# Nine layer norms in fp16 parts transposed by DMA, and the dense weight split early, in a one-core transformer block

## The chip, the core and the metric

The kernel runs on one core of a Trainium2 chip: TensorE (PE in the rows, its weight loads PEld), VectorE (DVE), ScalarE (ACT), GpSimd (POOL), and SyncE (SP), which here only issues DMAs. The metric is device time in microseconds (us) of one execution, as the median of several.

## The reference, cut to what matters

```python
def _layernorm(x): return (x - mean(x)) / sqrt(var(x) + 1e-5)
def _binary_diff_weight(w, base): d = w - base; return base + mean(abs(d)) * sign(d)
def ffn(h):   # W1, W3: [1792, 512], W2: [512, 1792], each from _binary_diff_weight
    return (silu(h @ W1.T) * (h @ W3.T)) @ W2.T
x = x + 0.5 * ffn(_layernorm(x))          # x: [2, 1024, 512] float32
x = x + attn(_layernorm(x))               # qkv, rope, causal softmax, dense; 32 heads, 8 kv heads of 16
x = x + 0.5 * ffn(_layernorm(x))
```

## The kernel before

The 2048 tokens are 16 tiles of 128 rows, in 4 chunks of 512. Every layer norm of a chunk has a number n: 0 to 3 feed the chunks of the first FFN, 4 to 7 the qkv projection, 8 to 11 the second FFN. Float32 products are made of three fp16 products (`PASSES`), each operand being a high part (the value rounded to fp16) and a low part (what the rounding left).

A norm goes like this. `norm_stats` on VectorE makes mean and 1/sigma of four token tiles (four `BN_STATS` and some 17 tiny steps). `normalised` writes four tiles `xnorm` in float32, a token on each partition. The products need the features on the partitions, so `ln_transpose` on TensorE transposes each tile by four 128x128 products with `ident` into PSUM; `ln_hi` on ScalarE casts a bank to the high part in `xt`, `ln_lo` on VectorE subtracts it and writes the low part.

A step t of an FFN chunk (14 of them, `IT`) is `gate(t)`, `up(t)` and then `down(t-1)` on TensorE, 12 products each. ScalarE follows with `silu` and `h_hi`, VectorE with `product` and `h_lo`. The next chunk's norm stands between these: stats and `normalised` after step 1, the transposes around the gate of step 12; norms 4, 5 and 6 lie around steps 4, 8 and 12 of the first FFN's last chunk (`LN_AT`).

The qkv stage loops over 16 token tiles. TensorE makes `qkv(i)` into one of two PSUM pairs; `take_raw(i)` on ScalarE empties it, and TensorE waits for that of tile i-2 before tile i. GpSimd makes `rot_s` (the sine half of the rotation), VectorE `along(i)` (the cosine half), `add_turned(i)` and `low_parts(i)`, ScalarE `high_parts(i)`. Norm 7 sits in this loop: its stats after pass 2 of VectorE's loop, `normalised` after pass 4, transposes ahead of `qkv(6)` and `qkv(7)`. SyncE then transposes q and k parts by DMA into `qa` and `ka` (`place_operands(g)`), in program order on its one queue.

Attention is a hand-written order over 16 groups g and periods k: `score_piece(k, r)` on TensorE and `reduce_piece(k, r)` on VectorE find each row's maximum of group k (25 pieces), the transposed maxima are copied to `mrow` (`take_rowmax`) and four DMAs put them as rows into `qa`, and one and two periods later the scores of that group, with `exps` on ScalarE and `values` on TensorE. TensorE's `scores_t(g, 0, 0)` waits for the four `mrow` DMAs (`m_placed`).

The dense weight is loaded behind the operands of group 2 (`wd_raw`), its largest magnitude taken by ScalarE in period 0 (`dense_magnitude`), reduced over partitions by GpSimd (`dense_bound`), turned into a power of two by VectorE between pieces 16 and 17 of period 0 (`dense_scale`), its high parts cast by ScalarE (`dense_high`), its low parts subtracted by GpSimd (`dense_low`); four DMAs `wd_at` to `wd` follow in period 7, on SyncE between `place_operands(10)` and the `mrow` DMAs of group 8.

Of the kernel before, what the change touches and what calls it, by code (L numbers as in the profile page):

```python
# [123 lines left out]
def build(nc, x_in, w1t, m1t, w3t, m3t, w2t, m2t, wqkvt, b_qkv, wdt, b_d, cos_in, sin_in, out):  # L124
# [143 lines left out]
    lnt_full = sem("lnt_full")  # L268
    xhi_ready, xlo_ready = sem("xhi_ready"), sem("xlo_ready")
# [18 lines left out]
    wd_scaled, wd_unit, wdhi_ready, wdlo_ready, wd_placed = (  # L288
        sem("wd_scaled"), sem("wd_unit"), sem("wdhi_ready"), sem("wdlo_ready"), sem("wd_placed"))
# [43 lines left out]
    LN_AT = {4: 4, 8: 5, 12: 6}  # L333

# [22 lines left out]
    def _(sp):  # L357
# [35 lines left out]
        sp.dma_start(bq[:, :], b_qkv.partition_broadcast(P)).then_inc(tables_loaded, 16)  # L393

# [15 lines left out]
        sp.wait_ge(lnt_full, 8 * TPC)  # L410
# [6 lines left out]
        sp.dma_start(wd_raw[:, :, :], wdt.rearrange("(t p) n -> p t n", p=P)).then_inc(wd_loaded, 16)  # L417
        sp.dma_start(bd[:, :], b_d.partition_broadcast(P)).then_inc(wd_loaded, 16)
# [1594 lines left out]
```

## Time and profile before

| | |
|---|---|
| time, median of 3 | 1526.37 us (1523.14 to 1528.73) |
| the profiled execution: its time, its span | 1523.47 us, 1521.7 us |
| TensorE busy | 1428.3 us, 94% of the span |
| VectorE, ScalarE, GpSimd busy | 57%, 40%, 11% |
| mean granted TensorE clock | 0.977 of full speed |
| first FFN from its chunk 1; qkv; attention; second FFN | from 154.5, 489.5, 571.1, 1073.9 us |

A share of busy time is a mean over stages. TensorE is busy throughout both FFNs; between 571 and 632 us it is busy in part only, at half clock.

### The profile page before, as it was taken

What the parts mean: (1) busy time and instruction counts of PE and PEld (TensorE: products, weight loads), DVE (VectorE), ACT (ScalarE), POOL (GpSimd) and SP (SyncE); (2) the same over time, 40 slices, a digit from 0 to 9 for tenths busy, and PEclk for the clock granted to TensorE, in tenths of its full rate; (3) what the DMA queues carried; (4) which work ended last, traced back from release to release, by engine and by line L of the source; (5) the groups of instructions that cost most, each with busy time, mean ns of one, the idle gap of its engine ahead of it and who ended that gap; (6) DMA issues with size and microseconds to landing.
All of it is one profiled execution on the core that took longest, in us unless ns stands there. A gap on an engine that the chain in (4) does not pass through costs nothing.

```text
span 1521.7 us, 24288 instructions
## 1 busy us (share of the span) xinstructions
PE 1428.3 (94%) x9136; PEld 628.1 (41%) x9136; DVE 865.0 (57%) x1362; ACT 601.9 (40%) x852; POOL 167.8 (11%) x251
## 2 busy tenths in 40 slices
PE   1999999999999993799999999999999999999998
PEld 0444444444444451233333333334444444444443
DVE  7998414413453766899998999945412412412212
ACT  5862112212221452477777778753212112112111
POOL 1000000000000650233332222210000000000000
PEclk9999999999999995699999999999999999999999
DMA  9605500000000013011112111024000000000000
GB/s 387 224 0 191 234 0 1 0 0 1 1 0 1 1 30 75 1 31 27 28 28 61 26 28 26 2 98 194 0 0 0 28 0 1 28 0 1 28 0 28
DMA packets 64136, 68.88 MB, mean 45 GB/s; under 512 B 52016, under 2 KB 52016, under 8 KB 63536
## 3 DMA queue, kind: packets, MB, share of 16 engines
q1 hardware_dynamic: 64048, 67.67, 13.1%
q8 instruction: 60, 0.98, 0.3%
q14 instruction: 28, 0.23, 0.1%
HBM read 40.63 MB, written 15.20 MB: 37 GB/s over the span
## 4 chain that ended last, share of the span: by engine, by line
PE 88%; DVE 4%; issue 3%; SPq 2%; DMA 1%; ACT 1%; POOL 0%; DVEq 0%; ACTq 0%; POOLq 0%
PE ps L1504 38%; PE ps L1525 17%; PE ps L1743 9%; PE ps L1657 6%; PE ps L1724 5%; PE ps L1644 4%; PE ps L1841 3%; PE ps L1551 2%; PE ps L1498 1%; PE ps L1753 1%; DVE rowmax L1332 1%; DMA w_raw<-w1t 1%; PE ps L1661 1%; SPq L403 1%; SPq L399 1%
## 5 line engine op out<-in xcount | busy, mean ns | idle before, releaser
L803 ACT ACTIVATE probs<-ps 128x1024 f32<-128x1024 f32 (+3 forms) x384 | 292.2, 812 | 85.1 <-PE ps L1724 83.5
L1504 PE MATMUL ps<-xt_hi,w_all 128*128 128x512 f16 x896 | 275.3, 380 | 9.3 <-DVE w_all L1011 9.3
L1332 DVE TENSOR_REDUCE rowmax<-ps 128x2 f32<-128x1024 f32 (+3 forms) x208 | 237.4, 1142 | 12.4 <-PE ps L1665 5.9
L1657 PE MATMUL ps<-ka,qa 48*128 48x512 f16 (+3 forms) x768 | 162.6, 347 | 36.8 <-DVE rowmax L1332 22.6
L1166 DVE SCALAR_TENSOR_TENSOR hb<-ps,scal,silub 128x512 f32<-128x512 f32 x56 | 42.0, 750 | 267.4 <-PE ps L1504 267.4
L1504 PE MATMUL ps<-xt_lo,w_all 128*128 128x512 f16 x448 | 170.5, 381 | 0.0
L1743 PE MATMUL ps<-probs,vs 128*32 128x512 f32 (+3 forms) x1536 | 165.4, 502 | 2.4 <-ACT ctx_sb L822 2.4
L1336 DVE TENSOR_REDUCE rowmax<-ps 128x1 f32<-128x512 f32 x192 | 131.1, 683 | 8.1 <-PE ps L1657 8.1
L1504 PEld LDWEIGHTS ps<-xt_hi,w_all 128*128 128x128 f16 (+1 forms) x896 | 87.9, 98 | 115.1 <-issue 11.4
L1724 PE MATMUL ps<-qa,ka 50*128 50x512 f16 (+3 forms) x768 | 131.8, 331 | 3.2 <-DMA qa<-mrow 2.3
L1525 PE MATMUL ps<-w32b_all,hhib 128*128 (+1 forms) x448 | 133.3, 379 | 0.0
L1166 DVE SCALAR_TENSOR_TENSOR ha<-ps,scal,silua 128x512 f32<-128x512 f32 x42 | 31.5, 751 | 153.5 <-PE ps L1504 153.5
L715 ACT ACTIVATE silub<-ps,scal 128x512 f32<-128x512 f32 x56 | 38.5, 687 | 197.9 <-PE ps L1504 197.9
L536 POOL TENSOR_SCALAR_AFFINE_SELECT probs<-probs 128x512 f32<-128x512 f32 x128 | 81.6, 637 | 309.5 <-ACT probs L803 309.5
L1657 PEld LDWEIGHTS ps<-ka,qa 48*128 48x128 f16 x768 | 48.9, 95 | 154.0 <-DVE rowmax L1332 84.2
L1525 PE MATMUL ps<-w_all,hhia 128*128 128x512 f16 (+1 forms) x336 | 100.0, 379 | 0.0
L722 ACT CAST hhib<-hb 128x512 f16<-128x512 f32 x56 | 34.6, 617 | 157.8 <-DVE hb L1166 157.8
L1525 PE MATMUL ps<-w32b_all,hlob 128*128 (+1 forms) x224 | 84.9, 379 | 0.0
L715 ACT ACTIVATE silua<-ps,scal 128x512 f32<-128x512 f32 x42 | 28.9, 687 | 140.4 <-PE ps L1504 140.4
L722 ACT CAST hhia<-ha 128x512 f16<-128x512 f32 x42 | 25.9, 617 | 117.2 <-DVE ha L1166 117.2
L1504 PE MATMUL ps<-xt_hi,w32b_all 128*128 128x512 f16 x224 | 71.2, 379 | 0.0
L1504 PE MATMUL ps<-xt1b_hi,w32b_all 128*128 128x512 f16 x224 | 71.2, 379 | 0.0
(164 smaller groups left out, 2090.5 us busy)
## 6 DMA issues: line engine op xcount, KB each, us to landing
spill<-w_all SPq DMA_DIRECT2D x1, 10752.0 KB, 29.0
w32b_all<-spill SPq DMA_DIRECT2D x1, 7168.0 KB, 20.7
x<-x_in SPq DMA_DIRECT2D x4, 1024.0 KB, 5.4
y_out<-x SPq DMA_DIRECT2D x4, 1024.0 KB, 4.2
wbase<-m1t SPq DMA_DIRECT2D x4, 896.0 KB, 12.8
w_raw<-w1t SPq DMA_DIRECT2D x4, 896.0 KB, 14.4
wbase<-m3t SPq DMA_DIRECT2D x4, 896.0 KB, 24.5
w_raw<-w3t SPq DMA_DIRECT2D x4, 896.0 KB, 24.4
```

The costliest lines, as they stand in the source:

```text
L536: nc.gpsimd.affine_select(out=p, in_=p, compare_op=ALU.is_ge, fill=0.0, base=0, pattern=[[0, Q_PER_KV], [1, P]], channel_multiplier=-1).th ...
L715: nc.scalar.activation(bufs["silu"][u][:, :], ps[:, GATE, :], ACT.Silu, scale=scal[:, 0:1])\
L803: nc.scalar.activation(probs[u % PBUF][:, 2 * pair:2 * pair + 2, 0:q1 - q0], wide(("scores", g, (u, pair)))[:, :, 0:q1 - q0], ACT.Exp, sca ...
L1166: nc.vector.scalar_tensor_tensor(out=bufs["h"][u][:, :], in0=ps[:, UP, :], scalar=scal[:, 1:2], in1=bufs["silu"][u][:, :], op0=ALU.mult, o ...
L1332: nc.vector.tensor_reduce(dst, src, AX.X, ALU.max).then_inc(pair_taken, 1)
L1336: nc.vector.tensor_reduce(rowmax[:, slot, kind, j:j + 1], ps[:, SINGLE_BANK, 0:w], AX.X, ALU.max)\
L1504: last = mm(ps[:, bank, :], w[a][:, k, bass.ts(t, P)], xt[b][:, k, :], start=(k == 0 and n == 0), stop=(k == HB - 1 and n == 2))
L1525: last = mm(ps[:, DOWN + j, :], hs[a][:, j * P:(j + 1) * P], w[b][:, t, :], start=(first and n == 0), stop=(last_tile and n == 2))
L1644: last = mm(ps[:, 2 * (i % 2) + s, 0:QKV // 2], xt[a][:, k, j * P:(j + 1) * P], wq[b][:, k, s * QKV // 2:(s + 1) * QKV // 2], start=False, ...
L1657: return mm(ps[:, bank, off:off + w], qa[g % BUF][64 * b:64 * b + ROWS, j, qt * P:(qt + 1) * P], ka[g // 2 % BUF][64 * b:64 * b + ROWS, k0 ...
L1724: last = mm(bank[:, b, 0:q1 - q0], ka[g // 2 % BUF][64 * b:64 * b + MROWS, kt * P:(kt + 1) * P], qa[v][64 * b:64 * b + MROWS, pair, q0:q1] ...
L1743: last = mm(ps[32 * h:32 * h + 32, CTX_BANK, at:512], vs[g // 2 * 2 % BUF + h % 2][:, kt, :], probs[u % PBUF][:, h, 0:q1 - q0], start=firs ...
```

## The change

It has two parts.

1. Norms 2 to 7 and 9 to 11 no longer touch TensorE or ScalarE. For each token tile VectorE (`normal_parts`) writes the normalised tile to a float32 temporary, casts it to the high part and subtracts for the low part, both fp16 and token-major in the tile `xnorm`; each of the three instructions waits for the one before. SyncE (`place_normal`) then issues one DMA transpose of 128x512 for each part, eight for a norm. In the FFNs the parts are made two tiles behind step 2 and two behind step 3, and for norms 4 to 6 at the corresponding steps; in qkv one tile ahead of each of passes 3, 4, 5 and 6 of VectorE's loop. Norms 0, 1 and 8 stay as they were (`ON_PE`).
2. The dense weight is loaded after the qkv weight in the first FFN, its bound taken by VectorE in chunk 1, high parts cast by ScalarE in chunk 2, low parts made by VectorE at the end of chunk 2; both are stored in HBM (`spill_d`, 1 MB) and loaded back behind the operands of group 3. The steps of periods 0, 1 and 7 are gone.

```diff
+    xtemp = {n: at(f"xtemp{n}", [P, HID], F32, a) for n, a in ((2, B0 + 57344 + 11264), (7, B0 + 32768), (9, 49152))}
+    wd_all = at("wd_all", [P, 2, HB, HID], F16, R0)
+    spill_d = nc.dram_tensor("spill_d", [P, 2 * HB * HID], F16)
+    ON_PE = (0, 1, 8)
+    def ln_placed_by(eng, n):
+        earlier = [i for i in range(n + 1) if i not in ON_PE and i % 2 == n % 2]
+        eng.wait_ge(ln_placed[n % 2], 16 * 2 * TPC * len(earlier))
+    def ln_parts(j):
+        t = xnorm[j][:, :].bitcast(F16)
+        return t[:, 0:HID], t[:, HID:2 * HID]
...
+        def place_normal(n):
+            for j in range(TPC):
+                sp.wait_ge(xhi_ready, TPC * n + j + 1)
+                sp.wait_ge(xlo_ready, TPC * n + j + 1)
+                for i in range(2):
+                    sp.dma_start_transpose(xt_of(n)[i][:, :, j * P:(j + 1) * P], ln_parts(j)[i])\
+                        .then_inc(ln_placed[n % 2], 16)
...
+        sp.wait_ge(up_full, IT)
+        place_normal(2)
+        sp.wait_ge(up_full, 2 * IT)
+        place_normal(3)
+        sp.wait_ge(wdhi_ready, 1)
+        sp.wait_ge(wdlo_ready, 1)
+        sp.dma_start(spill_d.ap(), wd_all[:, :, :, :].rearrange("p s a b -> p (s a b)")).then_inc(wd_spilled, 16)
+        sp.wait_ge(up_full, 3 * IT)
+        place_normal(4)
+        sp.wait_ge(wlo_ready, 3 * SLICES + 1)
+        place_normal(5)
+        place_normal(6)
+        sp.wait_ge(up_full, 4 * IT)
+        place_normal(7)
...
-        sp.wait_ge(lnt_full, 8 * TPC)
+        ln_placed_by(sp, 7)
         place_operands(0)
...
-        sp.dma_start(wd_raw[:, :, :], wdt.rearrange("(t p) n -> p t n", p=P)).then_inc(wd_loaded, 16)
-        sp.dma_start(bd[:, :], b_d.partition_broadcast(P)).then_inc(wd_loaded, 16)
...
         place_operands(3)
+        sp.wait_ge(wd_spilled, 16)
+        sp.dma_start(wd_all[:, :, :, :].rearrange("p s a b -> p (s a b)"), spill_d.ap()).then_inc(dense_loaded, 16)
+        sp.dma_start(bd[:, :], b_d.partition_broadcast(P)).then_inc(dense_loaded, 16)
...
-            if g == 7:
-                sp.wait_ge(wdlo_ready, HB)
-                for i in range(2):
-                    for n in range(2):
-                        sp.dma_start(wd[i][:, 2 * n:2 * n + 2, :], wd_at[2 * i + n][:, :, :]).then_inc(wd_placed, 16)
...
+        def normal_parts(n, j):
+            if j == 0:
+                if n in (2, 9):
+                    dve.wait_ge(lnt_full, on_pe(n - 1, TPC - 1))
+                else:
+                    ln_placed_by(dve, n - 1)
+            t = xtemp[max(i for i in xtemp if i <= n)]
+            hi, lo = ln_parts(j)
+            if j or n not in (2, 7, 9):
+                dve.wait_ge(xlo_ready, TPC * n + j)
+            nc.vector.tensor_scalar(t[:, :], x[:, TPC * (n % 4) + j, :], mean_var[:, n % 4, j, 0:1],
+                                    rstd[:, n % 4, j:j + 1], ALU.subtract, ALU.mult).then_inc(xnorm_ready, 1)
+            dve.wait_ge(xnorm_ready, TPC * n + j + 1)
+            nc.vector.tensor_copy(hi, t[:, :]).then_inc(xhi_ready, 1)
+            dve.wait_ge(xhi_ready, TPC * n + j + 1)
+            nc.vector.tensor_tensor(out=lo, in0=t[:, :], in1=hi, op=ALU.subtract).then_inc(xlo_ready, 1)
...
         for i in range(TOKEN_TILES + 1):
-            if i in (6, 7):
-                ln_lo(7, 2 * (i - 6))
-                ln_lo(7, 2 * (i - 6) + 1)
+            if 3 <= i < 7:
+                normal_parts(7, i - 3)
...
-            if i == 4:
-                normalised(7)
...
-            if k == 0:
-                dense_scale()
...
         for i in range(TOKEN_TILES):
-            if i in (6, 7):
-                ln_transpose(7, 2 * (i - 6))
-                ln_transpose(7, 2 * (i - 6) + 1)
             qkv(i)
```

On TensorE, at step 12 of chunk 1 of the first FFN (`xnorm_70` to `_73` are the four tiles of norm 2, `xt` chunk 1's operand), before:

```order
L1498 MATMUL ps<-ident,xnorm_70 128x128 x4
L1498 MATMUL ps<-ident,xnorm_71 128x128 x4
L1504 MATMUL ps<-xt_hi,w_all 128x512
L1504 MATMUL ps<-xt_lo,w_all 128x512
L1504 MATMUL ps<-xt_hi,w_all 128x512 x2
```

and now:

```order
L1600 COMPARE_AND_BRANCH
L1529 MATMUL ps<-xt_hi,w_all 128x512
L1529 MATMUL ps<-xt_lo,w_all 128x512
L1529 MATMUL ps<-xt_hi,w_all 128x512 x2
L1529 MATMUL ps<-xt_lo,w_all 128x512
```

Eight transposes ahead of the gate are gone, and as many behind it; nothing takes their place on this engine.

On VectorE, in the qkv loop around norm 7 (`rot`: the rotated tile, `parts_q` and `parts_k`: its low parts), before, passes 4 to 6:

```order
L945 TENSOR_SCALAR xnorm_72<-x,mean_var,rstd 128x512
L945 TENSOR_SCALAR xnorm_73<-x,mean_var,rstd 128x512
L1286 TENSOR_TENSOR rot_109<-rot_109,rot_s 128x640
L1279 TENSOR_TENSOR rot_110<-qkv_raw_108,cos 128x640
L1293 TENSOR_TENSOR parts_q<-rot_109,parts_q 128x32x16
L1295 TENSOR_TENSOR parts_k<-rot_109,parts_k 128x8x16
L955 TENSOR_TENSOR xt_lo<-ps,xt_hi 128x4x128 x2
```

and now, from the end of the stats to pass 4:

```order
L930 TENSOR_SCALAR rstd<-nw 128x4
L964 TENSOR_SCALAR xtemp_75<-x,mean_var,rstd 128x512
L967 CAST xnorm_70<-xtemp_75 128x512
L969 TENSOR_TENSOR xnorm_70<-xtemp_75,xnorm_70 128x512
L1323 TENSOR_TENSOR rot_113<-rot_113,rot_s 128x640
L1316 TENSOR_TENSOR rot_114<-qkv_raw_112,cos 128x640
L1330 TENSOR_TENSOR parts_q<-rot_113,parts_q 128x32x16
L1332 TENSOR_TENSOR parts_k<-rot_113,parts_k 128x8x16
L964 TENSOR_SCALAR xtemp_75<-x,mean_var,rstd 128x512
```

Three instructions for a tile stand ahead of each of four passes, in place of four `TENSOR_SCALAR` at once and twice two subtractions.

On SyncE, behind the operands of group 10 in period 7, before:

```order
L439 DMA wd_hi<-wd_at_134 128x1024
L439 DMA wd_hi<-wd_at_135 128x1024
L439 DMA wd_lo<-wd_at_136 128x1024
L439 DMA wd_lo<-wd_at_137 128x1024
L429 DMA qa_120<-mrow 1x16x128 x4
```

and now:

```order
L456 DMA_TRANSPOSE ka_129<-parts_k 128x1x128
L483 DMA qa_124<-mrow 1x16x128 x4
L452 DMA_TRANSPOSE qa_127<-parts_q 128x2x128 x8
L483 DMA qa_125<-mrow 1x16x128 x4
```

The maxima of group 8 follow the operands directly.

## Rows read from the trace of the kernel before

**Rows 1.** The page: the span, and the last chain's shares by line.

```profile
span 1521.7 us, 24288 instructions
...
PE ps L1504 38%; PE ps L1525 17%; PE ps L1743 9%; PE ps L1657 6%; PE ps L1724 5%; PE ps L1644 4%; PE ps L1841 3%; PE ps L1551 2%; PE ps L1498 1%; PE ps L1753 1%; DVE rowmax L1332 1%; DMA w_raw<-w1t 1%; PE ps L1661 1%; SPq L403 1%; SPq L399 1%
```

**Rows 2.** The chain by time (start, us, what), first FFN, step 12 of chunk 1.

```profile
242.57 2.59 PE ps L1525 x12
245.16 0.87 PE ps L1498 x8
```

**Rows 3.** Timeline of VectorE (start, us, operation, [idle before <-releaser]), chunk 1.

```profile
166.96 2.46 DVE L904 BATCH_NORM_STATS2 stats<-x 128x6 f32<-128x512 f32 x4
...
172.46 1.91 DVE L945 TENSOR_SCALAR xnorm<-x,mean_var,rstd 128x512 f32<-128x512 f32 x4
...
188.38 0.75 DVE L1166 SCALAR_TENSOR_TENSOR ha<-ps,scal,silua 128x512 f32<-128x512 f32 x1 [5.63 <-PE ps L1504]
```

**Rows 4.** A stretch in qkv: length, busy time of each engine, granted clock, DMA share, GB/s.

```profile
524.00:526.00 2.00, 2.00 (x7) 0.76 (x5) 1.40 (x2) 1.54 (x4) 1.91 (x3) 0.50 0.00 0
```

**Rows 5.** Timeline of TensorE: first qkv tile, and norm 7's first transposes.

```profile
489.52 0.33 PE L1640 MATMUL ps<-brow,row_ones 64*128 64x384 f16 x1
...
521.13 1.11 PE L1498 MATMUL ps<-ident,xnorm 128*128 128x128 f32 x8 [3.68 <-DVE xnorm L945]
```

**Rows 6.** The chain by time: the two halves of the last qkv tile.

```profile
566.81 2.06 PE ps L1644 x12
569.13 2.07 PE ps L1644 x12
```

**Rows 7.** Timelines of VectorE, ScalarE and GpSimd in qkv: passes 3 and 4.

```profile
513.02 0.82 DVE L1286 TENSOR_TENSOR rot<-rot,rot_s 128x640 f32<-128x640 f32 x1
...
516.79 0.81 DVE L1286 TENSOR_TENSOR rot<-rot,rot_s 128x640 f32<-128x640 f32 x1
...
515.14 0.89 ACT L779 ACTIVATE qkv_raw<-ps,scal 128x768 f32<-128x768 f32 x1
...
514.00 2.12 POOL L505 TENSOR_TENSOR rot_s<-qkv_raw,sin 128x320 f32<-128x320 f32 x2 [5.37 <-DVE rot L1286]
```

**Rows 8.** Timelines of VectorE and ScalarE in period 0 of attention.

```profile
604.50 0.15 DVE L1379 COPY wc<-allr 128x1 f32<-128x1 f32 x1 [8.42 <-POOL allr L548]
...
605.90 1.22 DVE L1332 TENSOR_REDUCE rowmax<-ps 128x2 f32<-128x1024 f32 x1
...
601.95 1.91 ACT L827 ACTIVATE probs<-wd_raw 128x2048 f32<-128x2048 f32 x1 [24.57 <-DMA bd<-b_d]
```

**Rows 9.** Timelines of SyncE, TensorE and ScalarE, periods 7 to 9.

```profile
822.07 1.23 SPq L439 DMA_DIRECT2D wd_hi<-wd_at  x2
...
824.66 2.51 SPq L429 DMA_DIRECT2D qa<-mrow  x4
...
828.37 0.39 PE L1724 MATMUL ps<-qa,ka 50*128 50x512 f16 x2 [2.28 <-DMA qa<-mrow]
...
792.67 0.26 ACT L813 COPY mrow<-ps 64x128 f16<-64x128 f16 x1 [0.88 <-PE ps L1707]
...
817.11 0.26 ACT L813 COPY mrow<-ps 64x128 f16<-64x128 f16 x1 [0.88 <-PE ps L1707]
...
845.35 0.26 ACT L813 COPY mrow<-ps 64x128 f16<-64x128 f16 x1 [0.88 <-PE ps L1707]
```

**Rows 10.** Line 399: issue in ns (min/median/max), and landing.

```profile
L399 SPq DMA_TRANSPOSE qa<-parts_q x128: 1182/1247/2638, 542.8 to 934.8; - x128
...
DMA to landing us min/median/max: 2.3/2.4/5.1
```

**Rows 11.** Timelines of SyncE (first and last operand transposes of groups 0 to 3) and TensorE.

```profile
542.79 1.27 SPq L399 DMA_TRANSPOSE qa<-parts_q  x1
...
604.85 2.54 SPq L399 DMA_TRANSPOSE qa<-parts_q  x2
...
628.61 1.04 PE L1724 MATMUL ps<-qa,ka 50*128 50x512 f16 x4
```

More of the change, by code:

```diff
@@ L268, in build @@
     lnt_full = sem("lnt_full")
+    ln_placed = [sem(f"ln_placed{i}") for i in range(2)]
     xhi_ready, xlo_ready = sem("xhi_ready"), sem("xlo_ready")
@@ L487, in over_partitions @@
             nc.gpsimd.partition_all_reduce(allr[:, w, 1:2], part[:, w, 1:2], P, RMAX).then_inc(allr_ready, 1)
-        for w in range(4):
+        for w in range(3):
             over_partitions(w)
+        pool.wait_ge(part_ready, 4)
+        nc.gpsimd.partition_all_reduce(allr[:, 3, :], part[:, 3, :], P, RMAX).then_inc(allr_ready, 1)
         H2 = HEAD // 2
@@ L557, in _ @@
             mask_unit(k - 2, 8)
-            if k == 0:
-                dense_bound()
-            if k == 1:
-                for n in range(HB):
-                    dense_low(n)
+            if k == 2:
+                pool.wait_ge(dense_loaded, 32)
             if 2 <= k < 10:
@@ L751, in ffn @@
                 for t in (IT - 2, IT - 1):
-                    if t == IT - 2 and ln is not None:
-                        ln_hi(ln, 0)
-                        ln_hi(ln, 1)
                     silu(T0 + t, t % 2, bufs)
-                    if t == IT - 2 and ln is not None:
-                        ln_hi(ln, 2)
-                        ln_hi(ln, 3)
                     h_hi(T0 + t, t % 2, bufs)
@@ L971, in difference, with power_of_two @@
                                     op=ALU.subtract).then_inc(diff_ready, 1)
-        def power_of_two(w):
-            bound, e, s, inv = (wc[:, w, i:i + 1] for i in (1, 2, 3, 4))
-            tmp = wc[:, w, 5:6]
+        def power_of_two(row):
+            bound, e, s, inv, tmp = (row[:, i:i + 1] for i in (1, 2, 3, 4, 5))
             chain(nc.vector.tensor_scalar(bound, bound, 2.0 ** -30, None, ALU.max))
@@ L1239, in ffn @@
                             norm_stats(LN_AT[t + 2])
-                        if t + 1 in LN_AT:
-                            normalised(LN_AT[t + 1])
-                        if t in LN_AT:
-                            for j in range(TPC):
-                                ln_lo(LN_AT[t], j)
+                        for d in (0, 1):
+                            if t + 1 - d in LN_AT:
+                                normal_parts(LN_AT[t + 1 - d], 2 * d)
+                                normal_parts(LN_AT[t + 1 - d], 2 * d + 1)
                         product(T0 + t, t % 2, bufs)
@@ L1248, in ffn @@
                 if ln is not None:
-                    layer_norm(ln)
-                with dve.Fori(1, 6) as i:
+                    norm_stats(ln)
+                for t in (2, 3):
+                    product(T0 + t, t % 2, bufs)
+                    h_lo(T0 + t, t % 2, bufs)
+                    if ln is not None:
+                        normal_parts(ln, 2 * (t - 2))
+                        normal_parts(ln, 2 * (t - 2) + 1)
+                with dve.Fori(2, 6) as i:
                     for t in (0, 1):
@@ L1255, in ffn @@
                 for t in (IT - 2, IT - 1):
-                    if t == IT - 2 and ln is not None:
-                        for j in range(TPC):
-                            ln_lo(ln, j)
                     product(T0 + t, t % 2, bufs)
@@ L1576, in ffn @@
                         down(T0 - 1, IT - 1, 1, wc_, bufs, False, True)
-                if (f, c) == (0, CHUNKS - 1):
-                    for t in range(2, IT):
-                        if t in LN_AT:
-                            ln_transpose(LN_AT[t], 0)
-                            ln_transpose(LN_AT[t], 1)
-                        gate(T0 + t, t, wa, xt)
-                        if t in LN_AT:
-                            ln_transpose(LN_AT[t], 2)
-                            ln_transpose(LN_AT[t], 3)
-                        up(T0 + t, t, wb, xt)
-                        down(T0 + t - 1, t - 1, (t - 1) % 2, wc_, bufs, False, False)
-                    continue
                 with pe.Fori(1, 6) as i:
```

126 lines of the change are left out of this document (51 added, 75 removed).

## The prediction

> **What bounds the kernel now.** I read the page first, for the chain that ended last: over half of it is the FFN's products (lines 1504 and 1525), and line 1498, the transposes of the norms, stands in it with 1% of its own [rows 1]. So a transpose on TensorE costs its full length there. The chain in order of time then shows the size: between a down of step 11 and the gate of step 12 eight transposes take 0.87 us and nothing waits [rows 2]. Next I read the timelines of the places where the chain leaves TensorE. There are three. In qkv TensorE stands idle 3.68 us for norm 7's tiles and works at half clock behind that, 0.50 in the stretch shown [rows 4, 5]. In period 0 of attention VectorE, which sets the pace there, waits 8.42 us for GpSimd's bound of the dense weight, which waits for ScalarE, which waits for a DMA [rows 8]. In period 8 TensorE waits 2.28 us for the maxima, whose DMAs stood on SyncE behind the four of the dense weight [rows 9].
>
> **The FFNs.** Eight of the nine moved norms (2 to 6, 9 to 11) lie in them, each twice eight transposes: 16 x 0.87 = 13.9 us off the path. What comes in their place must hide. VectorE has 5.63 us idle in every step of 14, waiting for TensorE [rows 3]. After step 1 it now has the stats alone, 172.46 - 166.96 = 5.5 us, which just fits; before, the tiles of `normalised` (1.91 us) stood there too. After steps 2 and 3 it has two tiles' parts. I call the time of one p: the `TENSOR_SCALAR` is about 0.5 us (1.91 for four), the subtraction about 0.7, between that and the 0.75 of a comparable instruction [rows 3], and the cast is not in the trace. Its bounds are the 0.15 us of a one-column copy [rows 8] and 0.75; I take 0.54, as the `TENSOR_SCALAR` is nearest to it, and with three waits on its own results p = 1.9 (1.5 to 2.2). Two are 3.8 us and fit into 5.63. If they didn't, `product` would be late, and TensorE asks for it only after another down and gate, 5.2 us later by 2.59 us for 12 products [rows 2]; so there is as much cover again. The same cover takes the dense weight's new work: a reduce and a subtraction over 2048 columns on VectorE and a cast on ScalarE, about 2 us each by ScalarE's 1.91 for that width [rows 8]. I cost all of it at nothing.
>
> SyncE is idle in the FFNs. A transpose of 128x256 takes it 1.25 us to issue and 2.4 to land [rows 10]; those of 128x512 are not in the trace. At the same issue cost a norm takes 10 us, if both scale with size 20 us. A step is three times 12 products, 7.77 us [rows 2]. Norm 4 is ready 12 steps before qkv, at 489.5 - 93.2 = 396.3, and norms 9 to 11 some ten steps before their use, so either hides.
>
> The Trainium skill (Advanced Engine Details and Errata, X-Bar Transpose) says that DMA transposes on TRN2 are as fast as regular DMAs, 350 to 400 GB/s. By it the 128 KB move in an estimated 0.4 us and the issue stays the limit; that changes only the chance of the last rival below.
>
> **qkv.** The stage lasts from 489.52 to 571.20, 81.7 us; a tile's half is 569.13 - 566.81 = 2.32 us, so 16 tiles are 74.2 and 7.4 us are lost now (the idle time, two times eight transposes, the half clock) [rows 4 to 6]. In the changed order the loss comes from VectorE. The passes of its loop, when it is behind, are 516.79 - 513.02 = 3.77 us apart, and the copy of the tile after next is done 516.03 - 513.02 = 3.0 us after a pass begins [rows 7]. The stats end at 513.02 as before; then a part stands ahead of each of passes 3 to 6, so pass 6 begins at 513.02 + 4p + 3 x 3.77, and tile 9 of TensorE may begin 3.0 later, at 527.3 + 4p. Unhindered it would begin at 489.52 + 9 x 4.64 = 531.3. The loss is 4p - 4.0, for p = 1.9 it is 3.6, and the gain 3.8 (5.4 for p = 1.5, 2.6 for 2.2). From pass 7 on VectorE catches up. I take the clock as full, since this comes as four waits of under 1.5 us, where before one of 3.68 stood.
>
> The Trainium skill (VectorE: DVE Perf Modes, the perf-mode tier table) has float32 copies in SBUF at two elements a cycle, 1227 ns for 2048. By it the cast would be an estimated 0.4 us and the gain in qkv 4.3 us. No row shows a cast between SBUF tiles on VectorE.
>
> **Period 0.** VectorE's wait began at 604.50 - 8.42 = 596.08, and the next piece began at 605.90: 9.8 us with the tiny steps [rows 8]. VectorE alternates with TensorE there, at half clock, and found two banks filled after the wait; I take off 0.3 for that: 9.5 (8.4 to 9.8). The stage is otherwise unchanged, and comes 3.8 us earlier by qkv. What could be late next is SyncE's queue. It issues its operand transposes from 542.79 to 607.39 without a break, and TensorE needs the maxima of group 0 at 628.61 [rows 11]. Now tile 7's parts end at about 535.6 + 4p = 543.2, half a microsecond later, two loads (1.1 us) follow at the end instead of in between, where they stood before, and the use comes at 628.61 - 13.3 = 615.3. The queue is free at 607.9, the four DMAs take 828.37 - 824.66 = 3.7 us to their use [rows 9], so they are in time at 611.6, and even 2 us behind a loaded megabyte. Cost: nothing, 3.7 us to spare.
>
> **Period 8.** From copy to copy of the maxima a period is 24.44 us (792.67 to 817.11), and the one with the wait 28.24 [rows 9]: 3.8 us too long, more than the wait itself. The four DMAs took SyncE 824.66 - 822.07 = 2.6 us. Without them the maxima are usable at 825.8, and TensorE stood ready at 828.37 - 2.28 = 826.1. That is a margin of 0.3 only, so the bounds are 0 and 3.8; I take 3.6.
>
> **The sum** is 13.9 + 3.8 + 9.5 + 3.6 = 30.8 us. From the profiled execution, 1521.7 in span and 1523.5 in time, that gives 1490.9 and 1492.7. This execution lies 2.9 us under the median shown, so against the median I expect 1526.4 - 30.8 = 1495.6.
>
> **The rivals.**
> - GpSimd and VectorE block each other in qkv. GpSimd's products of a pass are 1.06 us each and run from 514.00 to 516.12, which is 1.0 to 3.1 us into a pass, and a part begins at 3.77 [rows 7]; that speaks against it. If each part waited for one, p = 3.0, the loss in qkv is 8.0 and its gain -0.6: 1500.0. The Trainium skill (SBUF — State Buffer, SBUF: two separate sides) says that a VectorE instruction using two ports and a GpSimd instruction exclude each other for a whole instruction; by it this is what the cast would meet. Chance 0.1.
> - The maxima of group 0 come behind the reloaded megabyte, whose landing takes longer than thought. From 3.7 us of lateness on TensorE waits for them, at most until the old 9.5 us are spent; for half of them, 1500.4. Against it: all other DMAs of that stretch are short. Chance 0.1.
> - Period 8 keeps its wait, as the margin is 0.3: 1499.2. Chance 0.1.
> - Slower: the DMA transposes of 128x512 are slow and serial. Norms 4 to 6 need 24 of them between 396.3 us and 513, where VectorE waits for norm 6 before it overwrites the tiles: 4.9 us each. Beyond that VectorE and with it qkv stand still, 24 us for every further microsecond, and from 4.9 + 30.8/24 = 6.2 us each the change loses. Twice the landing of the smaller ones, 4.8, would be just under the bound if nothing overlapped, but now one is issued every 1.25 us while each lands in 2.4 [rows 10], so they overlap. At 7 us each: 1546. Chance 0.04.
>
> **Chances and range.** Likeliest case 0.66, its own range 1492 to 1499. The first three rivals reach to 1500 one by one and to 1504 where two meet. Downwards, p = 1.5 and a fully returned period 8 give 1493.6, and the median of a few runs may be some 2.5 us off, as those of before are from 1523.1 to 1528.7. So 1490 to 1504. About 0.5% (8 us) is what a measurement tells from no change. All cases but the last are beyond it; for what I haven't seen I leave 0.03 in between: faster 0.93, same 0.03, slower 0.04.
>
> **What would show it.** Chunks 1 to 3 of each FFN without a gap, a step of 7.77 us throughout. In qkv, waits of about 1 us ahead of tiles 6 to 9, no half clock, and an end 3.8 us nearer to its start; a part on VectorE of 1.9 us. In period 0, pieces 16 and 17 adjacent. In period 8, 24.4 us. Wrong would be: DMA transposes landing after more than 5 us, TensorE waiting for `ln_placed` anywhere, or a first wait for the maxima of group 0.

## The result, and the profile after

The changed kernel takes 1491.80 us (median of four runs, 1491.60 to 1493.89), the kernel before, run beside it, 1526.86 us (1523.14 to 1528.73): a ratio of 0.9776, 95% interval 0.9756 to 0.9797, or 35 us less. The predicted time was 1495.6 us, from 30.8 us of gain. The profiled execution of the changed kernel took 1493.89 us, its longest; against the profiled one of before (1523.47 us) the gain is 29.6 us. The two gains differ because the one profile lies above its median and the other below; the experiments show in part where. One run each of norms_only (2887.66 us), of warm_queue (1843.58) and of before (1578.21), from the experiments below, stands far outside all others and is left out.

The page, its span and the last chain's shares, answers to [rows 1]: the norms' transposes, line 1498 before, are gone from the chain's shares (1529 and 1550 are the FFN's products, 1658 and 1725 the two kinds of scores), VectorE's reductions (1366) are further up.

```profile
span 1492.1 us, 24245 instructions
...
PE ps L1529 39%; PE ps L1550 17%; PE ps L1744 10%; PE ps L1658 7%; PE ps L1725 5%; PE ps L1648 3%; PE ps L1842 3%; PE ps L1576 2%; DVE rowmax L1366 2%; PE ps L1754 1%; PE ps L1662 1%; DMA w_raw<-w1t 1%; DVE rowmax L1370 1%; PE ps L1832 1%; ACT ctx_sb L847 1%
```

The chain by time, first FFN: between the downs and the next gate of a step that held 0.87 us of transposes [rows 2] nothing stands now.

```profile
239.88 3.67 PE ps L1529 x17
243.55 2.59 PE ps L1550 x12
246.14 3.88 PE ps L1529 x18
```

VectorE's timeline in qkv: the first part of norm 7, 1.65 us from its start to the first operation of the next pass (line 1323), and one pass later the first operation of the second part, which took 0.92 us in place of 0.55, and the pass behind it. The second part took 2.03 us (512.68 - 510.65); the third and fourth took 1.64 and 1.63.

```profile
505.25 0.55 DVE L964 TENSOR_SCALAR xtemp<-x,mean_var,rstd 128x512 f32<-128x512 f32 x1
505.82 0.43 DVE L967 CAST xnorm<-xtemp 128x512 f16<-128x512 f32 x1
506.29 0.69 DVE L969 TENSOR_TENSOR xnorm<-xtemp,xnorm 128x512 f16<-128x512 f32 x1
506.90 0.82 DVE L1323 TENSOR_TENSOR rot<-rot,rot_s 128x640 f32<-128x640 f32 x1
...
510.65 0.92 DVE L964 TENSOR_SCALAR xtemp<-x,mean_var,rstd 128x512 f32<-128x512 f32 x1
...
512.68 0.82 DVE L1323 TENSOR_TENSOR rot<-rot,rot_s 128x640 f32<-128x640 f32 x1
```

TensorE's longest wait in qkv, and the stretch around it (length, busy time of PE, PEld, DVE, ACT, POOL, then the granted clock, which stays at 1.00):

```profile
515.74 0.33 PE L1644 MATMUL ps<-brow,row_ones 64*128 64x384 f16 x1 [1.07 <-ACT qkv_raw L806]
```

```profile
514.00:516.00 2.00, 0.93 (x6) 0.29 (x4) 1.32 (x2) 1.97 (x4) 2.00 (x3) 1.00 0.64 130
```

The source view of the new DMA transposes (issue in ns, min/median/max, and landing in us). Beside those of 128x256 in [rows 10], twice the columns cost nearly the same to issue and to land.

```profile
L430 SPq DMA_TRANSPOSE xt_hi<-xnorm x28: 1189/1204/1348, 177.6 to 1190.7; - x28
L430 SPq DMA_TRANSPOSE xt_lo<-xnorm x28: 1251/1262/1271, 178.9 to 1192.0; - x28
...
DMA to landing us min/median/max: 2.4/2.5/4.0
```

Period 0, VectorE's pieces 16 and 17 (before 9.8 us apart [rows 8]) and the small steps behind piece 24:

```profile
581.58 0.68 DVE L1370 TENSOR_REDUCE rowmax<-ps 128x1 f32<-128x512 f32 x1
582.37 1.23 DVE L1366 TENSOR_REDUCE rowmax<-ps 128x2 f32<-128x1024 f32 x1
...
592.82 0.18 DVE L1381 TENSOR_TENSOR rowmax<-rowmax 128x16 f32<-128x16 f32 x1
593.03 0.19 DVE L1388 TENSOR_SCALAR nm<-rowmax 128x32 f16<-128x32 f32 x1
```

Those small steps took longer before (L1347 and L1354, the same two):

```profile
614.40 1.04 DVE L1347 TENSOR_TENSOR rowmax<-rowmax 128x16 f32<-128x16 f32 x1
615.48 1.09 DVE L1354 TENSOR_SCALAR nm<-rowmax 128x32 f16<-128x32 f32 x1
```

Both profiled executions by stage. "Copy n" is ScalarE's copy of group n's maxima (`mrow`); the interval 8 to 9 is what the prediction calls period 8.

| stretch | before | after | gain | predicted |
|---|---|---|---|---|
| both FFNs (10 and 6 times eight transposes) | | | 8.7 + 5.2 | 13.9 |
| first to last bias product of qkv | 79.27 | 74.96 | 4.3 | 3.8 |
| last bias product to copy 0 | 49.56 | 38.28 | 11.3 | 9.5 |
| copy 8 to 9 | 28.24 | 24.44 | 3.8 | 3.6 |
| copy 0 to 1 | 27.48 | 29.51 | -2.0 | 0 |
| copy 10 to 11 | 24.43 | 25.44 | -1.0 | 0 |
| start to chunk 1 of the first FFN | 154.5 | 155.5 | -1.0 | 0 |

With 0.2 us in other intervals these make the 29.6 us. The last row is not the change's: chunk 1 starts between 154.0 and 155.7 us in the thirteen profiled executions, at 155.6 in warm_queue and at 154.0 in all_four, whose instructions are the same up to there. No wait for `ln_placed` stands in the trace.

### The profile page after: what moved, and what is told of

The parts are those of the page before. It is cut to its first block, busy times and chain, and to the rows that moved or that the text cites. A ratio compares the mean times of both kernels' runs of the same rounds, so it can differ in the third digit from the quotient of the medians.

```text
span 1492.1 us, 24245 instructions
## 1 busy us (share of the span) xinstructions
PE 1412.3 (95%) x8992; PEld 611.6 (41%) x8992; DVE 887.0 (59%) x1399; ACT 579.6 (39%) x812; POOL 161.3 (11%) x245
## 4 chain that ended last, share of the span: by engine, by line
PE 90%; DVE 6%; ACT 1%; issue 1%; DMA 1%; SPq 0%; POOL 0%; DVEq 0%; ACTq 0%; POOLq 0%
PE ps L1529 39%; PE ps L1550 17%; PE ps L1744 10%; PE ps L1658 7%; PE ps L1725 5%; PE ps L1648 3%; PE ps L1842 3%; PE ps L1576 2%; DVE rowmax L1366 2%; PE ps L1754 1%; PE ps L1662 1%; DMA w_raw<-w1t 1%; DVE rowmax L1370 1%; PE ps L1832 1%; ACT ctx_sb L847 1%
## 5 line engine op out<-in xcount | busy, mean ns | idle before, releaser
L1529 PEld LDWEIGHTS ps<-xt_hi,w_all 128*128 (+1 forms) x896 | 88.1, 98 | 116.8 <-issue 12.4
L1550 PE MATMUL ps<-w_all,hhia 128*128 (+1 forms) x336 | 99.9, 379 | 0.0
L1529 PE MATMUL ps<-xt1b_hi,w1b_all 128*128 128x512 f16 x224 | 71.2, 379 | 0.0
L1529 PE MATMUL ps<-xt_hi,w1b_all 128*128 128x512 f16 x224 | 71.2, 379 | 0.0
```

Source lines behind the costliest of these rows:

```text
L1529: last = mm(ps[:, bank, :], w[a][:, k, bass.ts(t, P)], xt[b][:, k, :], start=(k == 0 and n == 0), stop=(k == HB - 1 and n == 2))
L1550: last = mm(ps[:, DOWN + j, :], hs[a][:, j * P:(j + 1) * P], w[b][:, t, :], start=(first and n == 0), stop=(last_tile and n == 2))
```

## The experiments

All times are medians. The kernels ran in several groups, the kernel before beside each, with medians of 1526.0 to 1527.3 us; differences of about 1 us between kernels of different groups are therefore weak evidence by themselves. The table gathers what the sections below use (us): the intervals come from the profiled executions, one for each kernel.

| kernel | time, range | last bias product to copy 0 | copy 0 to 1 | 8 to 9 | 10 to 11 |
|---|---|---|---|---|---|
| before | 1526.9 (1523.1-1528.7) | 49.56 | 27.48 | 28.24 | 24.43 |
| changed | 1491.8 (1491.6-1493.9) | 38.28 | 29.51 | 24.44 | 25.44 |
| norms_only | 1512.6 (1511.6-1512.7) | 53.75 | 28.09 | 29.39 | 25.28 |
| dense_only | 1511.1 (1510.7-1512.5) | 38.27 | 27.87 | 24.42 | 24.43 |
| scale_later | 1517.8 (1514.5-1519.6) | 39.49 | 28.50 | 29.79 | 24.42 |
| norms_scale_later | 1501.6 (1501.5-1505.5) | 42.55 | 27.69 | 29.30 | 25.48 |
| late_reload | 1496.9 (1493.0-1500.5) | 38.28 | 27.86 | 29.69 | 25.23 |
| norm7_pe | 1495.5 (1494.6-1496.2) | 38.28 | 27.82 | 24.44 | 24.45 |
| spread | 1491.7 (1490.3-1492.2) | 38.28 | 29.07 | 24.64 | 25.19 |
| warm | 1490.6 (1490.0-1491.7) | 36.03 | 29.17 | 24.43 | 24.44 |
| warm_queue | 1487.4 (1486.3-1488.2) | 36.03 | 24.93 | 24.42 | 24.42 |
| split_place | 1490.8 (1490.7-1490.9) | 38.27 | 27.95 | 24.42 | 24.42 |
| all_four | 1483.9 (1483.1-1485.3) | 36.03 | 24.93 | 24.43 | 24.43 |

### The two halves of the change: norms_only, dense_only

norms_only is the diff without everything that names `wd`, `wdc` or `dense`; dense_only is the rest of it on its own:

```
# norms_only keeps of before:                # dense_only keeps of before:
sp.dma_start(wd_raw..., wdt...)  # late      ln_transpose / ln_hi / ln_lo for all norms
dense_magnitude, dense_high, dense_scale     layer_norm(ln), normalised(n)
four copies wd_at -> wd at g == 7
```

> The kernel before with the nine norms moved, and the dense weight prepared in attention as before. Theory: the first FFN is shorter by five times 1.75 us, the second by three, qkv by 4.4 us, and the 8.4 us wait of VectorE in period 0 and the 2.3 us wait of TensorE in period 8 stay: 18 us under before, 1508 to 1509. Rival 1 (the parts do not add up, the norms also bring what the profiles show in period 0 beyond the stall): 20 us or more under before. Rival 2 (part of the shorter qkv is given back in the wait of period 0, which ends when a DMA ends and not when qkv does): 14 us under before.

> The kernel before with the dense weight's parts made in the first FFN, spilled, and reloaded, and every norm still transposed by TensorE. Theory: period 0 loses its stall of 9.8 us and the slow tiny steps (1.75 us), period 8 its 3.1 us, and 2.0 us are given back in period 1: 12.6 us under before, 1514. Rival (the 1.75 and the 2.0 belong to the norms): 13 us less the rest, the profile then shows the tiny steps at 1.0 us and period 1 at 27.5. A second rival, on the spread: before's runs lie 3 to 5 us above its profiled one and after's do not; if the load of the dense weight in attention makes that spread, this kernel's runs agree within 0.5 us and the median gains about 16.

norms_only is 14.0 us under the kernel before (ratio 0.9902, 0.9866 to 0.9939), not 18, and dense_only 15.5 (0.9895, 0.9866 to 0.9923). Together they make 29.5 us, the whole change 35.1: 5.6 us belong to neither part alone. norms_only shows whose 4.2 of them are; the other 1.4 us are of the size by which the medians of before differ between groups (1526.0 to 1527.3). Its qkv is as short as the changed kernel's (480.26 to 555.22, 74.96 us), but VectorE's wait in period 0 has grown from 8.42 us [rows 8] to

```profile
595.22 0.15 DVE L1424 COPY wc<-allr 128x1 f32<-128x1 f32 x1 [12.72 <-POOL allr L599]
```

and SyncE's timeline says why: the loads of the dense weight stand in its queue behind operand transposes of 1.25 us each that follow one another without a gap.

```profile
583.87 1.25 SPq L445 DMA_TRANSPOSE qa<-parts_q  x1
585.16 1.23 SPq L449 DMA_TRANSPOSE ka<-parts_k  x1
586.49 0.53 SPq L463 DMA_DIRECT2D wd_raw<-wdt  x1
587.06 0.51 SPq L464 DMA_DIRECT2D bd<-b_d  x1
```

The shorter qkv did not move this queue: its first operand transpose is issued 53.1 us behind the first bias product (533.34 - 480.26), in before 53.3 us (542.79 - 489.52). So the second rival of the expectation holds: the 4.3 us of qkv are given back (from last bias product to copy 0 it takes 4.2 us more) as long as the dense weight is loaded there.

dense_only was expected 12.6 us under before. It is 12.4 us under it in the profiled executions and 15.5 in the medians. The stall and period 8 came as expected, and the small steps take 0.17 and 0.19 us, so they belong to this half. Two stages did not: copy 0 to 1 gave back 0.4 us and not 2.0, and qkv took 80.58 us, 1.3 more than in before. Behind the same wait of TensorE (3.66 us) the clock was at 0.50 when it began again at 522.10; in before, where it began at 521.13, the window from 520 to 522 is at 1.00:

```profile
522.00:524.00 2.00, 1.90 (x8) 1.57 (x9) 2.00 (x5) 0.00 (x0) 0.00 (x0) 0.50 0.00 0
```

The rival on the spread is undecided: it named a median gain of 16 and runs within 0.5 us, and the runs lie 1.8 us apart (8.2 for those of before beside them).

### The stall alone: scale_later, norms_scale_later

```
         for k in range(GROUPS):
...
-            if k == 0:
-                dense_scale()
             reduce_piece(k, 17)
...
             split_rowmax(k)
+            if k == 0:
+                dense_scale()
# ScalarE: dense_high() goes behind take_rowmax(k - 1) at k == 1
```

> The kernel before with VectorE's dense_scale moved behind split_rowmax in period 0 and ScalarE's dense_high behind the copy of group 0's maxima in period 1; nothing else. Theory: the stall costs its full length in front of the end, so pieces 16 and 17 are adjacent, the copy of the maxima comes 9.8 us earlier and the kernel is 9.5 us faster than before (1517); ScalarE's 6.2 us of casts fit into the 11 us in which it has nothing. Rival (the time is given back in period 1, since the first scores wait for something else, such as SyncE's queue): 0 to 5 us faster, with a wait for the maxima of group 0.

> The kernel with the norms alone moved, and VectorE's dense_scale behind split_rowmax of period 0 (ScalarE's dense_high behind the copy of group 0's maxima). With the norms alone the wait of period 0 grew from 8.42 to 12.72 us and the shorter qkv brought nothing. Theory: the end of that wait was set by SyncE's queue, so the two parts of the gain are only had together: 14 us under the norms alone, 1498.5, which is the changed kernel and 5 to 6 us for period 8 and the slower small steps. Rival (qkv's gain is lost on something else in period 0): 1502 to 1503.

scale_later gains 8.9 us in the medians (0.9937, 0.9915 to 0.9959) where 9.5 were expected, and copy 0 comes 10.1 us nearer to qkv's end: 9.8 of the stall and 1.8 of the two small steps, which are short here too, less 1.4 for the steps of `dense_scale`, which now stand ahead of the copy. The stall did cost its full length, and a fix of a few lines in before's order of work would have had most of it. norms_scale_later was to give 1498.5 and gave 1501.6, 11 us under norms_only: the theory fell 3 us short, and the rival (1502 to 1503) was nearer. Against scale_later qkv is 5.1 us shorter and the stretch behind it 3.1 us longer, so most of qkv's gain is still lost there. VectorE still waits, now behind `split_rowmax`, because SyncE's queue has not moved:

```profile
596.37 0.15 DVE L1424 COPY wc<-allr 128x1 f32<-128x1 f32 x1 [2.97 <-POOL allr L599]
```

That wait and the steps behind it (1.4 us, to 597.76) make the 42.55 us against 38.28 of the changed kernel. With the interval 8 to 9 (4.9 us more) this accounts for 9.1 of the 9.8 us that the two kernels lie apart.

### Period 8: late_reload

```
-        sp.dma_start(wd_all[...], spill_d.ap()).then_inc(dense_loaded, 16)
...
                 place_operands(g + 3)
+            if g == 7:
+                for i in range(4):
+                    sp.dma_start(wd_all[:, i // 2, 2 * (i % 2):2 * (i % 2) + 2, :]..., spill_d.ap()[...])
```

> The changed kernel with the dense weight's reload as four DMAs on SyncE ahead of the maxima of group 8, where the four DMAs of before stood. Theory: period 8 takes 28 us instead of 24.4 and the kernel is 3.1 to 3.8 us slower than the changed one (1495.2 against 1491.8). Rival (the wait of period 8 came from the copies out of SBUF, or was ScalarE's or TensorE's own lateness in that period): no difference to the changed kernel.

The four DMAs bring the wait back, and it costs more than the 3.1 to 3.8 us expected: 5.1 us in the medians, 5.25 in the interval 8 to 9. TensorE's timeline and the windows from 800 us on (length, busy time of PE, PEld, DVE, ACT, POOL, then the granted clock) show the two halves of it:

```profile
805.23 0.61 PE L1728 MATMUL ps<-qa,ka 50*128 50x512 f16 x2 [2.91 <-DMA qa<-mrow]
```

```profile
802.00:804.00 2.00, 0.32 (x6) 0.10 (x4) 1.21 (x2) 0.00 (x0) 0.00 (x0) 0.89 0.78 281
804.00:806.00 2.00, 0.77 (x3) 0.34 (x4) 0.00 (x0) 0.12 (x1) 0.00 (x0) 0.50 0.26 54
806.00:808.00 2.00, 2.00 (x20) 1.26 (x20) 0.68 (x2) 1.44 (x2) 0.00 (x0) 0.50 0.25 52
808.00:810.00 2.00, 2.00 (x17) 0.31 (x11) 1.79 (x2) 1.30 (x2) 0.64 (x1) 0.50 0.17 33
```

The wait is 2.9 us; behind it TensorE works at 1.2 GHz (0.50) until about 810 us, busy nearly all the time from 805 on, and the interval is another 2.3 us longer. It is not before's wait to the letter, as these DMAs load from HBM: the maxima are used 4.5 us behind their first issue (805.23 - 800.75), 3.7 in before. But norms_only, scale_later and norms_scale_later, which have before's own four copies, take 29.3 to 29.8 us there too. The four runs of late_reload spread over 7.5 us, those of the changed kernel over 2.3.

### qkv: norm7_pe, spread

```
# norm7_pe
-    ON_PE = (0, 1, 8)
+    ON_PE = (0, 1, 7, 8)      # with normalised, ln_transpose, ln_hi, ln_lo of norm 7 as before
# spread
-            if 3 <= i < 7:
-                normal_parts(7, i - 3)
+            if i in (3, 4, 6, 8):
+                normal_parts(7, (3, 4, 6, 8).index(i))
```

> The changed kernel with norm 7, the one made during qkv, transposed by TensorE again (normalised, ln_transpose, ln_hi and ln_lo at tiles 6 and 7 as before). Theory: qkv goes back from 77.3 to 81.7 us with one wait of TensorE of over 3 us and a stretch at half clock, all else stays: 4.4 us over the changed kernel, 1496.2. Rival (the shorter qkv is given back behind it, since SyncE's queue of operand transposes and not TensorE sets the start of attention): within 1.5 us of the changed kernel.

> The changed kernel with norm 7's four parts ahead of VectorE's passes 3, 4, 6 and 8 instead of 3, 4, 5 and 6. Theory: VectorE gains 0.87 us on TensorE in each pass (4.64 less 3.77) and a part costs 1.65, so its largest lag falls from 4.9 to 3.3 us, of which 2.2 are covered: TensorE loses 1.1 us in qkv instead of 3.1, and the kernel is 2.0 us faster than the changed one (1489.8). Rival (SyncE starts the operand transposes later, as norm 7's last transposes come later, and period 0 gives it back): 0 to 1 us faster.

norm7_pe is 3.7 us over the changed kernel (4.4 expected, under 1.5 by the rival), and the bias products are 79.26 us apart, as before; the first wait of TensorE and the stretch behind it are back, the clock at 0.68 and 0.50:

```profile
513.51 1.12 PE L1529 MATMUL ps<-ident,xnorm 128*128 128x128 f32 x8 [3.67 <-DVE xnorm L953]
```

```profile
514.00:516.00 2.00, 2.00 (x11) 1.06 (x10) 2.00 (x4) 0.41 (x1) 0.29 (x1) 0.68 0.00 0
516.00:518.00 2.00, 2.00 (x7) 0.91 (x6) 1.31 (x2) 1.92 (x4) 2.00 (x3) 0.50 0.00 0
```

spread shortens qkv by 1.5 us (73.46 between the bias products), where 2.0 were expected; the first two parts still fall on neighbouring passes, and the wait of 1.07 us is still there. Its median is only 0.1 us below the changed kernel's, which is what the rival named, though not for the rival's reason: the stretch to copy 0 is as long as in the changed kernel (38.28). What is new is a wait of TensorE for the maxima of group 0, since SyncE's queue did not move with qkv:

```profile
605.06 1.03 PE L1725 MATMUL ps<-qa,ka 50*128 50x512 f16 x4 [0.73 <-DMA qa<-mrow]
```

How much of the 1.5 us it takes was not tried; all_four below has them in its qkv.

### What holds the half clock, and SyncE's queue: warm, warm_queue

```
+        def busy(n):
+            for _ in range(n):
+                nc.tensor.matmul(ps[:, CTX_BANK, :], ident16[:, :], parts_q[:, 0, 0:8, :]..., start=True, stop=True)
# busy(30) behind piece 1 of group 0; busy(4) behind each pair piece of k == 0 and, up to piece 12, of k == 1
# warm_queue, SyncE:
-        place_operands(3)
-        sp.dma_start(wd_all...); sp.dma_start(bd...)
         for g in range(GROUPS):
             ...   # the four DMAs of mrow
+            if g == 0:
+                place_operands(3)
+                sp.dma_start(wd_all...); sp.dma_start(bd...)
```

> The changed kernel with extra products of TensorE whose result nobody reads (identity by 512 columns, into the bank of the context before its first use): 30 after piece 1 of group 0, while TensorE waits 7 us for VectorE, and 4 after each pair piece of period 0 and of the first half of period 1. It tests what the half clock from 562 to 617 us costs. In five kernels so far period 1 (from the first copy of maxima to the second) takes 27.48, 27.87, 27.86, 28.09, 28.50 and 29.51 us, the later the granted clock is back at 1.00 behind the first copy (17.1, 18.1, 17.8, 18.9, 19.7, 22.1 us). Theory: with the clock at 1.00 throughout period 1 takes 24.5 to 25 and the kernel is 3 to 5 us faster than the changed one, with up to 3 more from VectorE's short waits in period 0 (1484 to 1489). Rival 1: period 1 is long for its own reason (the first scores wait for the first maxima), and the products only stand in the way: 0 to 3 us slower than the changed one. Rival 2: the extra products do not hold the clock, half-rate ones take 0.43 us each and delay the pieces: 10 us slower.

> The kernel with the extra products (label warm) and, on SyncE, the four DMAs of group 0's maxima ahead of group 3's operand transposes and of the dense weight's reload. In warm the clock stood at 1.00 until 604 us and period 0 was 2.2 us shorter, but TensorE then waited 2.30 us for the maxima, whose DMAs stood behind those transposes until 598.46, and the clock fell there. Theory: with the maxima in time the clock stays, and period 1 takes 24.5 to 25.5 instead of 29.2: 4 us under warm, 1486.5. Rival (period 1 has its own length of 28 to 29, whatever the clock and the queue): within 1 us of warm, 1490.

warm takes 1490.6 us, outside the 1484 to 1489 expected, and it is neither of the rivals: the clock is at 1.00 through period 0, which is 2.25 us shorter, but the interval from copy 0 to 1 hardly shrinks (29.17). TensorE now comes to the first scores earlier and waits, and the clock falls after all:

```profile
604.14 0.60 PE L1725 MATMUL ps<-qa,ka 50*128 50x512 f16 x4 [2.30 <-DMA qa<-mrow]
```

```profile
598.00:604.00 6.00, 3.46 (x28) 1.51 (x28) 3.38 (x5) 0.00 (x0) 0.00 (x0) 1.00 0.60 221
604.00:610.00 6.00, 5.47 (x34) 1.39 (x34) 3.74 (x4) 3.94 (x5) 1.28 (x2) 0.57 0.01 3
```

The maxima were copied at 591.74, but SyncE had group 3's transposes and the reload in front of them (first DMA at 598.46). warm_queue turns this order round. Copy 0 to 1 takes 24.93 us, the kernel 1487.4 us, 3.2 under warm (expected 4), and the clock stays at 1.00:

```profile
600.00:606.00 6.00, 4.75 (x40) 1.78 (x41) 5.05 (x7) 2.73 (x4) 0.65 (x1) 1.00 0.22 44
606.00:612.00 6.00, 6.00 (x64) 1.85 (x64) 5.61 (x8) 4.11 (x7) 1.91 (x3) 1.00 0.67 232
```

The products alone brought 1.2 us. The new order alone was not run; in the changed kernel's trace TensorE doesn't wait for these maxima, so little is to be expected of it, but that is argued and not shown. In both kernels a small wait for later maxima has moved: the intervals 4 to 5 and 12 to 13 take 25.55 and 24.93 us in warm, 25.36 and 24.92 in warm_queue, and 10 to 11 takes 24.4.

### The remaining small waits: split_place, all_four

```
-            for tt in range(SEQ_TILES):
+            for tt in range(first, last):
...
+            if 2 <= g < GROUPS - 2 and g % 2 == 0:
+                place_operands(g + 2, 6)
             if 1 <= g < GROUPS - 3:
                 sp.wait_ge(st_full, 2 * NU * g)
-                place_operands(g + 3)
+                place_operands(g + 3, 0, 6 if g % 2 else SEQ_TILES)
```

> The changed kernel with the 16 operand transposes that SyncE issues in every second period split: 12 before the maxima of the next group, 4 behind them. In odd periods these 16 take it 20.5 us from 7 us after the copy on, so the next maxima's DMAs come 5.1 us after their copy, and in one period (the one of 25.44 us) TensorE waited 0.91 us for them. Theory: every period takes 24.4 us, 1.0 us faster than the changed kernel (1490.8), and the small waits disappear. Rival (the waits come from elsewhere): the period of 25.4 us is still there.

> The changed kernel with norm 7's parts spread (label spread), the extra products and the early maxima of group 0 (warm_queue) and the split transposes (split_place). Theory: the gains add: 1.5 us in qkv, 2.2 in period 0, 4 in period 1 and 1.0 in the later periods, 8.7 us under the changed kernel, 1483. Rival (period 1 keeps its length): 1487.

The small wait of the changed kernel is this one, again for the maxima, whose DMAs are issued 5.1 us behind their copy at 844.39 (SyncE's timeline, then TensorE's):

```profile
848.23 1.24 SPq L456 DMA_TRANSPOSE ka<-parts_k  x1
849.52 2.49 SPq L483 DMA_DIRECT2D qa<-mrow  x4
```

```profile
854.29 0.39 PE L1725 MATMUL ps<-qa,ka 50*128 50x512 f16 x2 [0.91 <-DMA qa<-mrow]
```

split_place removes it: all intervals behind copy 1 are 24.4 us (the last one 23.7, as in every kernel), and its four runs lie within 0.11 us, against 2.3 of the changed kernel and 5.1 of before beside it. all_four takes 1483.9 us (1483 expected), ratio 0.9727 (0.9714 to 0.9741) to before, 8 us under the changed kernel, with the last bias product 73.45 us behind the first one, period 0 at 36.03, copy 0 to 1 at 24.93 and the later intervals as in split_place. It is the fastest of all kernels here.

## Why the prediction was right, step by step

- **FFNs, 13.9 us:** measured 14.0. The parts hid: two take VectorE 3.5 us behind step 2, and it still waits 2.16 us for the next product (the row below); the DMA transposes of 128x512 cost 1.20 and 1.26 us to issue and 2.5 to land, as the smaller ones. The slow-transposes rival was never near.

```profile
181.43 0.75 DVE L1184 SCALAR_TENSOR_TENSOR ha<-ps,scal,silua 128x512 f32<-128x512 f32 x1 [2.16 <-PE ps L1529]
```

- **qkv, 3.8 us:** measured 4.3 (0.5 more). The mechanism was right: four waits of at most 1.07 us in place of one of 3.7 us, and the clock at 1.00. Three parts took 1.63 to 1.65 us, not 1.9, above all because the cast took 0.43 and not 0.54; the second took 2.03. The Trainium skill (VectorE: DVE Perf Modes, the perf-mode tier table), from which an estimate of 0.4 us was cited, was nearer; the trace agrees with it. The loss formula holds: 3.0 us were lost (74.96 less 31 half tiles of 2.32), and the four parts together, 6.95 us, less its 4.0 are 2.95.
- **Period 0, 9.5 us:** the stall went as sized, 9.8 us by the rows; scale_later bears it out. The stretch gained 11.3 us; the term was undersized by the two small steps of VectorE (1.04 and 1.09 us before, 0.18 and 0.19 after). The prediction had both in its reach and didn't look behind piece 24.
- **The spare 3.7 us of group 0's maxima:** nothing was lost, but the step was wrong. From the first of the four DMAs to a use that waited for them it takes 604.14 - 598.46 = 5.7 us in warm and 605.06 - 599.45 = 5.6 in spread, not 3.7. That figure, from one place of before, was the shortest of all such waits in these kernels (3.7 to 5.7). In the changed kernel the DMAs are issued from 598.73 and used at 605.43, which leaves 1.0 us. spread moved TensorE forward there and it waited 0.73 us, warm moved it 3.6 us and it waited 2.30: in both the rival came true, for want of margin and without a late megabyte being shown.
- **Period 8, 3.6 us:** right in the profile (3.8), probably undersized in the medians (5.1 by late_reload). Before's profiled execution had the shortest such interval of the five seen: 28.24 against 29.3 to 29.8 in four other kernels. The clock was at 1.00 for the first 2 us behind its wait and at 0.50 from 830 us on, in late_reload at 0.50 at once.
- **"The stage is otherwise unchanged":** wrong for what follows it, though not for long. The clock comes back later behind copy 0 in some executions than in others, and the interval follows it: 17.1 us and 27.48 (before), 18.0 and 27.86 (late_reload), 18.9 and 28.09 (norms_only), 19.7 and 28.50 (scale_later), 22.1 and 29.51 (changed; the first number is from copy 0 to the granted clock's return to 1.00, from windows of 2 us). split_place has the same instructions there as the changed kernel, late_reload too but for the reload, and both take 27.9; so 1.6 of its 2.0 us belong to the profiled execution and not to the kernel.
- **The interval 10 to 11, 1.0 us:** not foreseen. Five kernels that make norm 7 in parts have it, warm and warm_queue have such waits in other intervals, norm7_pe has none, and split_place wins back 1.0 us in the medians. The prediction saw the thin margin of the maxima in period 8 alone. It is no later issue that brings the wait: before issues these DMAs as late (874.88, 5.1 us behind the copy at 869.77) and uses them without a wait 3.7 us on, at 878.60, where the changed kernel's are used 4.8 us behind the first issue (854.29 - 849.52). Why they took longer is open.
- **The medians:** 14.0 + 4.3 + 11.3 + 5.1, less 0.4 and 1.0 given back, are 33.3 of the 35.1 us. Of the 2 us left up to 1.3 may lie in qkv: with norm 7 on TensorE it took 79.26 to 80.58 us in four executions, and before's 79.27 is at the short end.
- **The total:** 1491.8 us lies within 1490 to 1504, and 0.2 us below the likeliest case's own 1492 to 1499. That the profiles' 29.6 us fall 1.2 beside the 30.8 is luck in part. Period 0 and qkv gave 2.3 us more than their terms, and some 4 us in the last three rows of the table, of which none was in the sum, took them back. One slip of the working: the lower bound 1493.6 should read 1493.8 (1495.6 - 1.6 - 0.2).
- **What the sum left out:** that the parts of the sum depend on each other. It was made as if each stood alone. qkv's term would have been lost to the longer stall, had the dense weight stayed.

Not settled: what makes the runs of before spread over 5 to 8 us. Three stages vary between executions of the same instructions: the start of chunk 1 (1.7 us between the extremes), the stretch at half clock in qkv (1.3) and the return of the clock behind copy 0 (1.6). Waits of TensorE for the maxima with a fallen clock behind them are a further likely cause, as split_place, without any, has 0.1 us and late_reload, with a long one, 7.5. But norms_only has that wait too, and its three runs lie within 1.1 us, so this is argued and not shown.

## What to carry to other kernels

An in-order queue that issues small DMAs is a path of its own: ask of each DMA on the critical way what stands ahead of it in the queue, before asking how long it flies, and take the flight from more than one place. Terms of a sum that share such a queue do not add; test the parts of a change one by one and together. Here the waits of TensorE of 1.9 to 3.7 us cost more than their length, as half clock followed them, and those of 0.3 to 1.1 us in qkv cost their length alone, so short waits spread out were cheaper than one long one. Work whose result nobody reads pays where TensorE idles between bound steps, but only if nothing else makes it wait.

## What the runs showed of the hardware

- DMA transposes out of SBUF cost SyncE 1.20 to 1.26 us to issue (medians) whether they move 128x128, 128x256 or 128x512 fp16 elements, and land 2.3 to 2.5 us later.
- GpSimd held VectorE up: before, the two small steps of VectorE (rows above) ended at 615.44 and 616.57 us, where the last two of GpSimd's four subtractions of 1.14 us ended, at some 615.4 and 616.5:

```profile
612.04 4.48 POOL L542 TENSOR_TENSOR wd_at<-wd_raw,wd_at 128x512 f16<-128x512 f32 x4 [7.10 <-issue]
```

In scale_later, with the same steps and the subtractions later, from 612.68 us on, they took their own time:

```profile
605.79 0.17 DVE L1347 TENSOR_TENSOR rowmax<-rowmax 128x16 f32<-128x16 f32 x1
605.99 0.19 DVE L1354 TENSOR_SCALAR nm<-rowmax 128x32 f16<-128x32 f32 x1
```

The Trainium skill (SBUF — State Buffer, SBUF: two separate sides) has this as an exclusive lock on a shared port pair for a whole instruction, between GpSimd and VectorE instructions in a two-port mode or, against a GpSimd instruction that reads SBUF, with two SBUF inputs; the trace agrees for the two steps. It may also be behind the one `TENSOR_SCALAR` of 0.92 us in place of 0.54, beside which GpSimd ran a small `TENSOR_SCALAR` (510.27 us) and a memset (510.78); the next of these, at 516.44, took 0.53 though a memset from 516.17 overlapped it.
- TensorE's granted clock was 0.50 (1.2 GHz) from some 562 to 617 us in the changed kernel, and 1.00 (2.4 GHz) throughout that stretch in warm_queue and all_four, where extra products fill its idle time. Behind a wait of 1.07 us in qkv it stayed at 1.00; behind those of 1.88 (norms_only), 2.28 [rows 9], 2.91 (late_reload) and 3.67 us (norm7_pe) it went to 0.50.
- The same four small DMAs of the maxima were used 3.7 to 5.7 us behind their first issue, where a product waited for them.
